# The local attention products of a segment scan as eight block diagonal 128x128 products, one step later

## The reference, cut to what matters

```python
def step(carry, inp):
    mem, z = carry
    q_s, k_s, v_s, qn_s, kn_s = inp
    scores = jnp.einsum('bhnd,bhmd->bhnm', q_s, k_s) * SCALE
    scores = jnp.where(mask, scores, -jnp.inf)
    sdpa = jnp.einsum('bhnm,bhmd->bhnd', jax.nn.softmax(scores, axis=-1), v_s)
    sq = elu1(qn_s)
    num = jnp.einsum('bhnk,bhkv->bhnv', sq, mem)
    den = jnp.einsum('bhnk,bhk->bhn', sq, z)[..., None]
    mem_out = num / (den + 1e-06)
    out = beta * mem_out + (1.0 - beta) * sdpa
    sk = elu1(kn_s)
    prev_v = jnp.einsum('bhnk,bhkv->bhnv', sk, mem) / jnp.einsum('bhnk,bhk->bhn', sk, z)[..., None]
    mem = mem + jnp.einsum('bhnk,bhnv->bhkv', sk, v_s - prev_v)
    z = z + sk.sum(axis=2)
    return ((mem, z), out)
```

## Time and profile before

| what | value |
|---|---|
| median of 3 runs | 3094.67 us (3094.19 to 3098.59) |
| the profiled execution, its own time | 3102.11 us |
| its span, first to last instruction | 3100.2 us |
| mean granted TensorE clock | 0.939 of full speed |
| PE busy | 2652.2 us, 86% of the span |
| DVE busy | 2513.5 us, 81% |
| ACT busy | 1875.5 us, 60% |
| POOL busy | 1760.1 us, 57% |

### The profile page before, as it was taken

The page is one execution under the profiler, slowest core; times in us unless marked ns, Lnnn a source line. Parts: engine busy times, 40 slices in busy tenths (PEclk is TensorE's granted clock), DMA queues, the critical chain, the costliest instruction groups (busy, mean ns, idle before and its releaser), DMA issues. The chain is left out here.

```text
span 3100.2 us, 127998 instructions
## 1 busy us (share of the span) xinstructions
PE 2652.2 (86%) x53041; PEld 1472.6 (48%) x53041; DVE 2513.5 (81%) x7598; ACT 1875.5 (60%) x3797; POOL 1760.1 (57%) x1988
## 2 busy tenths in 40 slices
PE   5887999999999999772431899999999999999998
PEld 2442333333333333372220566666666666666665
DVE  4678999999998999586606789888888888888887
ACT  5786999999999999630001455545455555555553
POOL 5883222222222222240063788888888888888886
PEclk9997999999999999995655999999999999999999
DMA  4676444444434443191023000000000000000000
GB/s 128 204 241 159 93 90 93 98 101 95 93 94 99 94 95 87 41 322 57 0 45 95 4 11 11 11 4 11 11 11 11 11 11 11 11 11 5 11 8 11
DMA packets 173628, 201.48 MB, mean 65 GB/s; under 512 B 31153, under 2 KB 134513, under 8 KB 172785
## 3 DMA queue, kind: packets, MB, share of 16 engines
q1 hardware_dynamic: 170480, 191.87, 24.0%
q0 software_dynamic: 2560, 1.35, 0.4%
HBM read 125.10 MB, written 67.24 MB: 62 GB/s over the span
## 5 line engine op out<-in xcount | busy, mean ns | idle before, releaser
L851 ACT ACTIVATE at_pA<-at_ps 128x512 f32<-128x512 f32 x1024 | 552.0, 615 | 55.3 <-DVE at_ps L903 48.8
L912 DVE CUSTOM_DVE_ANT_0 at_junk<-at_ps,w_cmask 128x512 f32<-128x512 f32 (+3 forms) x1024 | 463.2, 485 | 100.1 <-PE at_ps L754 92.5
L903 DVE TENSOR_TENSOR at_ps<-at_ps,w_ratio 128x128 f32<-128x128 f32 (+3 forms) x1024 | 450.9, 491 | 2.0 <-PE at_ps L748 0.5
L720 POOL TENSOR_SCALAR_AFFINE_SELECT at_pB<-at_pB 128x128 f32<-128x128 f32 x256 | 74.8, 292 | 637.1 <-ACT at_pB L857 634.9
L857 ACT ACTIVATE at_pB<-at_ps 128x512 f32<-128x512 f32 (+1 forms) x768 | 379.9, 532 | 52.5 <-PE at_ps L761 47.3
L2001 POOL TENSOR_TENSOR sc_rb<-sc_rb,v_sin 128x512 f32<-128x512 f32 x256 | 326.1, 1274 | 43.8 <-DVE sc_ra L2244 42.6
L2037 PE MATMUL sc_ps<-sc_xT,v_wqkv 128*128 128x512 f32 x512 | 287.6, 645 | 3.3 <-PEq L56 1.4
L748 PE MATMUL at_ps<-at_aq,at_ak 72*128 72x512 bf16 x1024 | 277.7, 387 | 0.7 <-DVE at_mx L912 0.4
L2201 ACT COPY sc_skN<-sc_ps 128x512 f32<-128x512 f32 x128 | 74.9, 586 | 320.3 <-PE sc_ps L2092 320.3
L761 PE MATMUL at_ps<-at_bq,at_bk 75*128 75x512 bf16 (+3 forms) x1024 | 265.5, 302 | 1.5 <-ACT at_pB L857 0.9
L1996 POOL TENSOR_TENSOR sc_sk<-sc_ee,sc_relu 128x512 f32<-128x512 f32 x128 | 164.8, 1288 | 172.3 <-ACT sc_ee L2192 172.3
(11 more groups left out here) (317 smaller groups left out, 5910.6 us busy)
## 6 DMA issues: line engine op xcount, KB each, us to landing
parts_scratch<-fr_parts SPq DMA_DIRECT2D x64, 384.0 KB, 4.1
at_bk<-parts_scratch SPq DMA_DIRECT2D x192, 96.0 KB
at_ak<-parts_scratch SPq DMA_DIRECT2D x192, 96.0 KB
v_scratch<-fr_v SPq DMA_DIRECT2D x32, 352.0 KB, 4.4
at_v<-v_scratch SPq DMA_DIRECT2D x32, 352.0 KB, 3.5
at_bq<-parts_scratch SPq DMA_DIRECT2D x128, 64.0 KB
at_aq<-parts_scratch SPq DMA_DIRECT2D x128, 64.0 KB
on_scratch<-at_on SPq DMA_DIRECT2D x32, 256.0 KB, 2.2
```

What stands on the lines that cost most here:

```text
L851: act.activation(pA[:, n % A_RING, j * S:(j + 1) * S], src, ACT.Exp).then_inc(exped, 1)
L903: dve.tensor_tensor(src[:, 0:wide], src[:, 0:wide], W["ratio"][:, S - wide:S], ALU.mult).then_inc(tilted, 1)
L912: ins = dve.tensor_tensor_reduce(junk[:, P * j * (j + 1) // 2:P * (j + 1) * (j + 2) // 2], src[:, col:col + wide], W["cmask"][:, S - wide: ...
```

## The change

Each pair's eight blocks of softmax weights are put on the diagonal of eight 128x128 matrices, and one matmul with a full 128x128 weight load takes the place of four with 32x32. The matrices stand in a new tensor `pB`, zeroed once before the scan and kept in two copies. Four copies per step on ACT (`place_blocks`), one for each group of 32 partitions, move the blocks of `pT` to their places on the diagonal; they stand behind the first `features` of the step. The product itself moves one step later (pair `s - 3`), and with it the pass L2271 on DVE, the two POOL additions to `uu` and `ol`, `turn_heads`, `project_out` and the copies of their results. On DVE the pass over the local product now stands behind the first `rope` of the step. Before, PE waited ahead of `local` for `pt`, the end of DVE's work on the sums; now it waits for the previous copy of turned heads, and for `pb` only in the first steps. The loop has one step more.

```diff
+        SIDE = B1
+        pB = sb("pB", [P, 2, GH, SIDE, SEG])
...
+                    dve.memset(pB[:], 0.0)
...
-        STEPS = PT + 5
+        STEPS = PT + 6
...
-                        p = s - 2
+                        p = s - 3
                         if inside(p):
                             new = uu[:, p % PAIRS, :, :, 0:DH]
                             wait(pool, "kd", p + 1)
...
-                        p = s - 2
+                        p = s - 3
                         if inside(p):
                             wait(pool, "qd", p + 1)
                             wait(pool, "old", p + 1)
...
                     def local(p):
                         for g in range(BG):
                             for hh in range(2):
-                                for f in range(B1):
-                                    ch = 2 * g + hh
-                                    ins = pe.matmul(ps[32 * f:32 * f + 32, 6, ch * DH:(ch + 1) * DH], pT[32 * f:32 * f + 32, p % 4, ch, :],
-                                                    uu[32 * f:32 * f + 32, p % PAIRS, g, hh, 0:DH], start=True, stop=True)
+                                ch = 2 * g + hh
+                                for first in range(0, P, SIDE * SEG):
+                                    rows = slice(first, first + SIDE * SEG)
+                                    ins = pe.matmul(ps[rows, 6, ch * DH:(ch + 1) * DH], pB[rows, p % 2, ch].rearrange("p f j -> p (f j)"),
+                                                    uu[rows, p % PAIRS, g, hh, 0:DH], start=True, stop=True)
                         ins.then_inc(G["pvd"], 1)
...
-                        p = s - 2
+                        p = s - 3
                         if inside(p):
-                            wait(pe, "otc", min(s - 3, PT))
-                            wait(pe, "pt", p + 1)
+                            if s > 4:
+                                wait(pe, "otc", s - 4)
+                            else:
+                                wait(pe, "pb", p + 1)
                             local(p)
...
-                            wait(pe, "old", min(s - 1, PT))
+                            wait(pe, "old", min(s - 2, PT))
                             wait(pe, "sgk", p + 1)
                             turn_keys(p)
                         p = s - 1
                         if inside(p):
+                            if s < 3:
+                                wait(pe, "mu", 2 * min(s - 5, PT - 1) + 2)
                             wait(pe, "add_d", 2 * p + 2)
                             score(p)
...
+                        p = s - 5
+                        if inside(p):
+                            project_out(p)
                         p = s - 4
                         if inside(p):
-                            project_out(p)
-                        p = s - 3
-                        if inside(p):
...
+                    def place_blocks(p):
+                        wait(act, "pt", p + 1)
+                        wait(act, "pvd", p - 1)
+                        for f in range(B1):
+                            ins = act.copy(pB[32 * f:32 * f + 32, p % 2, :, f % SIDE], pT[32 * f:32 * f + 32, p % 4])
+                        ins.then_inc(G["pb"], 1)
...
                         if s < PT:
                             features(2 * s)
+                        p = s - 2
+                        if inside(p):
+                            place_blocks(p)
...
                     for s in range(STEPS):
-                        p = s - 2
+                        if s < PT:
+                            rope(2 * s)
+                        p = s - 3
                         if inside(p):
                             wait(dve, "pvd", p + 1)
-                            wait(dve, "pt", p + 1)
+                            wait(dve, "smd", p + 1)
...
                             wait(dve, "se", p + 1)
-                            dve.transpose(pT[:, p % 4].rearrange("p c j -> p (c j)"), ss[:, p % 2].rearrange("p c j -> p (c j)"))
+                            wait(dve, "pb", p - 3)
+                            dve.transpose(pT[:, p % 4].rearrange("p c j -> p (c j)"), ss[:, p % 2].rearrange("p c j -> p (c j)")).then_inc(G["pt"], 1)
...
-                            dve.reciprocal(s_, s_).then_inc(G["pt"], 1)
+                            dve.reciprocal(s_, s_).then_inc(G["smd"], 1)
```

More of the change, by code:

```diff
@@ L1801, in scan @@
         names = ("h_in0 h_in1 stat fact shift_d xn_d tq_d xnn_d xq_d step xt xt_c xqt xqt_c hb_d ffn ffn_c vp v_c pj ex mn rp sn sgq sgk add_d sS skt skc "
-                 "sx se pt pvd old kr_s qr_s kd ud qd od up mu ott otc oproj yt_c yt ydone stored0 stored1").split()
+                 "sx se pt smd pb pvd old kr_s qr_s kd ud qd od up mu ott otc oproj yt_c yt ydone stored0 stored1").split()
         G = {n: sem(n) for n in names}
@@ L1961, in turn @@
                     user(("xq", j), "xqt_c", j)
-                if s - 12 in starts:
-                    user(("y", (s - 12) // PAIRS), "ydone", (s - 12) // PAIRS + 1)
+                if s - 13 in starts:
+                    user(("y", (s - 13) // PAIRS), "ydone", (s - 13) // PAIRS + 1)
                 if s - 7 in starts:
@@ L2167, in _ @@
                             turn_xq(pe, bank_of("xq", j), j)
-                        if s - 12 in starts:
-                            j = (s - 12) // PAIRS
+                        if s - 13 in starts:
+                            j = (s - 13) // PAIRS
                             free_bank(pe, "y", j)
@@ L2213, in _ @@
                             features(2 * s + 1)
-                        p = s - 4
+                        p = s - 5
                         if inside(p) and p % PAIRS == PAIRS - 1:
@@ L2218, in _ @@
                             act.copy(yT[:], ps[:, 7, :]).then_inc(G["yt_c"], 1)
-                        p = s - 3
+                        p = s - 4
                         if inside(p):
@@ L2273, in _ @@
                             ins.then_inc(G["old"], 1)
-                        if s < PT:
-                            rope(2 * s)
                         if s < PT:
```

## The result

The changed kernel takes **3115.24 us** (median of five runs, 3110.97 to 3121.99); the kernel before, run beside it, 3094.67. But the terms of the sum did not come out as written. One was less than half of its real size, a loss of nearly the same size was missing, and the two cancelled: that the time fits so well is luck.

What follows compares the result with a forecast made beforehand. PE was taken to bound the kernel, DVE close behind, with 9.7 us of work in a 10.76 us step. 0.74 - 0.2 - 0.09 - 0.23 = +0.22 us per step, x 128 = 28, and 3: +31, 3126 us; range 3070 to 3162.

Steps and rivals of the forecast that it cites:

- local product: On PE, 16 matmuls with 128-column weight loads take 1.78 us in place of 1.04: +0.74 us per step.
- neighbours and the wait for the sums: Query projection and values gain a full width neighbour, -0.2; PE no longer waits for `pt`, -0.09 us per step.
- program blocks: PE's program arrives in blocks of about 127 matmuls, 3.6 us each; fewer matmuls end a third of stops: -0.23 us per step.
- cheap-loads rival: 64 columns with wide loads at 0.08 us each, local product 1.3 us, 0.48 less per step: 3065 us; chance 0.05.
- the "issue" time nearly vanishes: PE's stops with no releaser to be seen: forecast about a third lower; nearly vanishing or staying would prove the prediction wrong.
- the first rival: Also "All stops go": PE's queue runs ahead during the slow product, -0.75 us per step for stops: 3060 us; chance 0.21.
- Copies, order on DVE: ACT copies covered by its wait for turned keys, cost nothing; DVE's later pass nothing, bound 0.1 us per step.
- wait of the turned keys for `sc_ol`: PE waiting there for DVE's late pass would prove the prediction wrong; a new wait of 0.4 us per step: 3177 us.
- The extra step: The added last step puts one product and its pass behind the end: +3 us once.

Runs made afterwards that it cites:

- Run 7: Kernel before, its own order, with sixteen 64x64 local products a step, weights straight from `pT` (not the reference's sum): 3063.0 us, ratio 0.9885.
- Run 8: Changed kernel with the rounding of x divided, its first two DVE operations one step earlier: 3079.0 us, ratio 0.9938 to the changed kernel's predecessor.
- run 6: Kernel before, its own order, with eight 128x128 local products a step, weights straight from `pT` (not the reference's sum): 3115.7 us, ratio 1.0053.
- run 2: Changed kernel's order of steps, but with the 64 narrow local products out of `pT` and no ACT copies: 3104.8 us, 1.0019 to the kernel before.
- run 5: Changed kernel with blocks of 64x64 instead of 128x128, sixteen local products a step: 3088.4 us, 0.9974 to the kernel before.
- Run 1: Changed kernel with the turn and projection of y one step later still, 14 steps behind instead of 13: 3124 us, 1.0076 to the kernel before.
- run 9: Changed kernel with 64x64 blocks and the rounding of x divided over two steps: 3049.5 us, 0.9830 to the kernel before.
- run 10: Changed kernel with 64x64 blocks, divided rounding, and DVE scaling the local product ahead of `rope` again: 3032.8 us, 0.9775 to the kernel before.
- run 11: Kernel before with the rounding of x divided and nothing else: 3088.0 us, ratio 0.9958.
- run 4: Changed kernel with 48 more matmuls a step, 32x32 bf16 weights and 2 columns: 3315.5 us, 1.0688 to the kernel before.

## Why the prediction was right in the time and wrong in two of its steps

The sum per step beside the mean start-to-start time of PE's groups (records of 1800 to 3060 us, after minus before):

| step of the prediction | forecast | measured |
|---|---|---|
| local product | +0.74 | +0.65 (1.10 to 1.74) |
| neighbours and the wait for the sums | -0.29 | -0.16 (projections -0.12, values -0.04) |
| program blocks (recalls, scores, update, small groups) | -0.23 | -0.50 |
| a long step in eight (turned heads +0.12, turned y +0.07, turned x +0.01) | none | +0.20 |
| sum | +0.22 | +0.18 |

- **The local product** was nearly right: 1.73 / 16 = 0.108 us per load, for an estimated 0.111. (The Trainium skill, "TensorE: Matmul & The Clock Gate", section "LDWEIGHTS (loading the stationary operand)", gives a load its columns divided by 1.2, in nanoseconds: 107 for 128. The trace agrees. The 81 that the cheap-loads rival cited doesn't hold for this product.)
- **The neighbours** gained less than 0.2. The values went from 1.06 to 1.01, not to 0.96. The query projection ahead of the product, with its wait, went from 1.21 to 0.96 behind an update, but to 1.39 in the step with turned y.
- **The program's blocks: the step that failed.** "What matters is how long PE works on a block, against 3.6" took each block by itself, and left a block as short as 2.1 us to stop PE in any case. The prediction named the sign of its being wrong here, that the "issue" time nearly vanishes, and so it came: 63.5 us became 5.7, and the term was -0.50, not -0.23. Run 7 contradicts it too: a tenth fewer matmuls ended 87% of the stops. What the runs show in its place is that the mean decides. A step of the kernel before needs 342 / 127 = 2.69 blocks, and its 10.76 us leave 4.0 for each, about the 3.9 at which every kernel with many stops stands; the changed one needs 2.31, which leaves 4.7. Short blocks are made up for by long ones (49 us of shortfall, 4.4 of stops), so PE's supply does run ahead. That was the first rival's mechanism. (The Trainium skill, "Runtime: NRT & Kernel Launch", section "Instruction fetch mechanics", has crossing a block mostly hidden. The changed kernel agrees, with 5.7 us in all; the kernel before, with 63.5, doesn't. The rule holds here as long as the blocks of a step need less time than the step.) The prediction also read too few stops: its rows left out the 12.2 us ahead of the scores and some small ones, so that 0.50 per step is listed and not 0.36.
- **The rival's time** was wrong as well. "All stops go" was to give 3060, and 0.75 us per step was at stake. About 0.5 went, and something else came.
- **What came: the long step.** The prediction read DVE's wait at the update (26.7 us) as something that stays. It grew to 37.4, and PE's clock fell behind it eight times instead of three. Run 8 shows the cause of both: the rounding of x on DVE ahead of the pass that PE waits for. Of the growth, the rounding itself offers a cause: POOL's additions now stand beside it in nearly every segment (14 us, above). The new order alone does not explain that: of the two runs in the old order, run 6 has 29.8 us of this wait and no long L1633, but run 7 has 49.2 us and fifteen. It hangs on when DVE and POOL meet. That is argued from these rows; no run moved POOL alone. Where PE is quicker the wait grows further: 43 to 49 us in runs 2, 5 and 7.
- **The turned y** now stands between turned x and the next projection, and the two free banks of PSUM alternate, so that the projection needs the bank that x leaves: 2.8 us of listed wait for `sc_xT`, and 0.5 us more from y to projection in each eighth step. Run 1 moved y away and gained nothing, since the next step grew instead.
- **Copies, order on DVE.** The copies were covered. The wait of the turned keys for `sc_ol`, named as what would make the prediction wrong, came at 7.9 us or 0.06 per step, within the bound of 0.1. Without the slow product it is 38 to 43 us (runs 2, 5, 9), and the order on DVE is its cause (run 10).
- **The extra step** was to cost 3 us. Transposes and span give -5: the head and the first eight intervals are together 4.6 us shorter, and the tail 0.2.

What stays open: what sets the 3.9 us of a block and how far ahead blocks can come, how much of the longer wait is POOL's, and why the clock falls behind some of the long waits and not behind others.

## What to carry to other kernels

Where an engine stops for its own program, compare a mean: blocks of a loop times the time of a block, against the loop's length. Here a step that left 4.0 us for a block was full of stops, and with a tenth fewer matmuls (4.3 us) 87% of them were gone. Below that, a shorter wait may pay less: run 11 gained 12 us where the changed kernel gained 36, but it also had less of the wait to lose.

A stop that goes away uncovers the next engine. Before pricing it, look for waits at a fixed distance (sixteen in 128 steps): they belong to work that comes once in so many steps, and dividing that work (run 8) was worth twice what the whole change cost.

Choose the size of a block diagonal by the time of the product as well as by the count of instructions: 64x64 kept the product at 1.08 us and ended the stops just the same.

## What was not expected of the hardware

Two of the four rounding operations on DVE take 0.42 and 0.69 us alone, and up to 1.3 and 1.64 when a POOL addition is already under way. They then end at a fixed distance behind POOL, about 0.28 us for L1630 and 0.55 for L1633 in every long case of both kernels: DVE stands until POOL is done. L1633 is that long in 6 of its 16 cases before, and in 14 of 16 in the changed kernel. Where it began first it kept its 0.69 us, though the two ran side by side for up to 0.65; then it was POOL's addition that took longer, 1.60 to 1.78 us in the five cases where it came at most 0.22 us later, and else 1.26 to 1.37. (The Trainium skill, "SBUF — State Buffer", section "SBUF: two separate sides", has DVE and POOL share a pair of ports under an exclusive lock for the whole instruction. The trace agrees in these rows.)

PE's granted clock fell to its lower level for some microseconds behind waits of about 2 us (0.54 in 2282.5 to 2286.2), and never in the same stretch once the wait was at most 1.0 us (run 8). In the run with 64x64 blocks, whose waits are up to 3.0 us, it fell fourteen times between 1750 and 3050 us, and not once there with the divided rounding (run 9). But long waits are not the only thing that it falls behind: in run 4, whose waits at the update are at most 1.1 us and whose steps hold 48 matmuls of two columns more, it fell 36 times. No run shows why.

48 matmuls of two columns in one corner of the array take 1.17 us, 24 ns each, while the narrow product, spread over four corners, takes 1.04 us for 64 with 64 columns each, 16 ns. So few columns don't make a matmul cheap by themselves. That the shared corner is the reason is not shown: the 48 also differ from the narrow product in type and in place of output, and no run spread them over four corners.
